# A new opening and tail for a vision block: moved steps, a load order, a last block without its means

## The chip, the core and the metric

The kernel runs on one core of a Trainium2 chip. The metric is the device time of one execution in microseconds (us). TensorE (PE) multiplies matrices and writes only to PSUM; VectorE (DVE), ScalarE (ACT) and GpSimd (POOL) work elementwise; SyncE (SP) issues most DMA transfers. The engines run their own streams of instructions and wait for each other by semaphores.

## The reference

For each of 4 images (64 channels, 64x64): a 1x1 convolution to 16 channels, batch norm and relu, then a 1x1 convolution to 9 filters for each pixel, with which the 3x3 neighbourhood of each channel is summed (`h`, 4096 tokens of width 64). Then

```
h = h + attention(layernorm(h))        # one head of width 64, softmax over 4096 keys
y = layernorm(h)
e = argmax(y @ router_w.T + router_b)  # 32 experts, the best one for each token
h = h + relu(relu(y @ W1[e] + b1[e]) @ W2[e] + b2[e])
```

All in float32.

## The kernel before

**Blocks and groups.** The tokens of an image are cut into 4 blocks of 1024 queries (BT = 8 tiles of 128), 16 blocks in all (BLOCKS), numbered through the images. A block of attention is 16 groups (PAIRS); a group scores one pair of key tiles against the 1024 queries (`score`, 16 TensorE records, two units, each followed by an exponential on ScalarE) and weighs the values with the result (`into_z`, 16 records). `usual_score(n, g)` runs one group ahead of `usual_weigh(n, g - 1)`. In blocks 0 and 1 the work is interleaved (`attention`): block 0 handles the first 8 key pairs for queries 0 and 1, so that few keys are needed early. Pairs 0 to 3 are the keys of token block 0, pairs 4 to 7 those of token block 1.

**Fills.** Everything else is a named step `name@block`, placed in a group by hand (`opening_groups` to `last_groups`; group -1 is ahead of the first). Each engine walks the same list in the same order and does its part of each step, so a step in an engine's stream holds up whatever stands behind it. `cc`, `cv`: the two convolutions for a whole image. `sum0` to `sum2`: three filter taps each on VectorE, then `ln`, the LayerNorm, which writes the keys. `xt`: the keys transposed on TensorE (`turn`), copied by ScalarE; `g`: the keys times Wq Wk, used as queries. After a block of attention: `z` (VectorE adds the two halves), `pz` (times Wv, with a 65th column for the softmax sum), VectorE divides, adds the residual and normalises to `y_block`; `yt` transposes it, `lg` makes the router's logits, `first_best` the one-hot choice, `ot` transposes that, `hid0` to `hid3` are the first layers of the 512 hidden rows with the mask of the choice, `o2` the second layer, `fin` turns the result back and `put_out` adds it to `h2`.

**Places.** A fill writes to a place in PSUM: place 0 is `both` (2 banks of 512), 7 and 8 are the two score banks, 9 is `z_ps` (`AT_THE_END`, used in the last two blocks, when attention needs them no more). `wait_free` waits until the fill that held the place before is read out.

**The end.** Block 14's experts and all of block 15's run after the last weighing. For the last block the means are taken as in every block (`normalise`: sum, centre, square, sum, a reciprocal root in eight small operations), `lg` is copied by ScalarE to `logits` before VectorE looks at it, and `o2` is accumulated in two halves of PSUM (`h` = which 64 hidden rows), which ScalarE copies and VectorE adds.

**The opening.** TensorE starts on the first image's quarter, keeps busy with `warm` matmuls on ones, and then branches on a flag (`shift_if_needed`: whether scores need a shift against overflow; here they don't). The steps behind the branch stand far off in its stream, in the Else. SP issues the loads in one order; filters go through DRAM (`store_filters`) and come back spread over the channels in three thirds (`spread_filters`), into a ring of two slots and a spare one (`chosen`). SP holds the second and third third of block 1 back until TensorE is through its branch:

```
spread_filters(1, [0])
sp.wait_ge(asked_first, 1)
spread_filters(1, [1, 2])
store_filters([2, 3])
load_image(1, 0, TILES + 2, x_loaded[1])
```

Of the kernel before, what the change touches and what calls it, by code (L numbers as in the profile page):

```python
# [17 lines left out]
D = W  # L18
# [48 lines left out]
NONE = ("sum", "ln", "pow", "z", "ask", "warm", "pre", "out")  # L67
# [5 lines left out]
AT_THE_END |= {f"{name}@{BLOCKS - 1}": k for name, k in (("hid0", 7), ("hid1", 8), ("hid2", 9), ("hid3", 7), ("o2", 8))}  # L73
# [3 lines left out]
WARM_UP, STAY_WARM, KEEP_WARM = 8, 10, 10  # L77
# [22 lines left out]

def begins(n, g):

    return g == 0 or n < 2 and g == HALF
# [48 lines left out]
def usual_groups(n):  # L152
# [5 lines left out]
                    {8: at(m, "ot"), 9: at(i, "xt"), 10: [*at(i, "g"), *at(j, "sum0 sum1")]})  # L158
    if m in CHOSEN_BY_DMA:
# [42 lines left out]
def vit_block_kernel(nc, x, once, kept, out):  # L202
# [6 lines left out]
    with ExitStack() as ctx:  # L209
# [59 lines left out]
        wv_w = sb("wv_w", [128, 130])  # L269
        wqk = sb("wqk", [64, 2, 128])  # L270
# [43 lines left out]
        lower_copied, out_ready = sem("lower_copied"), sem("out_ready")  # L314
        choices_stored, choices_loaded = sem("choices_stored"), sem("choices_loaded")
# [72 lines left out]
        def _(sp):  # L388
# [4 lines left out]
            def store_block(m):  # L393
# [3 lines left out]
                else:  # L397
                    sp.wait_ge(drained[places.of[fin]], places.nth[fin])
                for half in range(HH):
                    rows = out.rearrange("b (c h q t) w -> b q h c (t w)", c=C, h=HH, q=NQ)  # L400
                    sp.dma_start(rows[m // NQ, m % NQ, half, :, :],
                                 out_sb[half * C:(half + 1) * C, m % 2, :, :].rearrange("c t w -> c (t w)")
                                 ).then_inc(out_stored[m % 2], 16)
# [100 lines left out]
            for k in range(2):  # L504
                sp.wait_ge(out_stored[k], 32 * BLOCKS // 2)

        @block.gpsimd
        def _(pool):
# [66 lines left out]
            P.tensor_tensor(router_w[:, :], load["rm"], load["rb"], ALU.subtract)  # L575

# [8 lines left out]
        def _(pe):  # L585
# [27 lines left out]
            def turn(tiles, ident=ident):  # L613

                for j in range(BT // 2):
                    for h in range(2):
                        for a in range(2):
                            last = T.matmul(both[rows_of(a), h, j * 64:(j + 1) * 64], tiles[2 * j + a][rows_of(h)],  # L618
# [11 lines left out]

            def begin_hidden(full):
                name, i = split(full)
                wait_free(full)
                wait_drained(f"yt@{i}")
                from_both(place[places.of[full]], w1, y_t, int(name[3:]), start=True, stop=False)

            def fill(full):
# [7 lines left out]
                elif name.startswith("pre"):  # L645
                    begin_hidden(f"hid{name[3:]}@{i}")
                if name.startswith(NONE):
# [29 lines left out]
                elif name == "cv":  # L677
# [8 lines left out]
                    last.then_inc(done, 1)  # L686
                elif name in ("xt", "yt"):
# [9 lines left out]
                    last.then_inc(done, 1)  # L697
                elif name == "g":
# [10 lines left out]
                    last.then_inc(done, 1)  # L709
                elif name == "pz":  # L710
                    pe.wait_ge(z_copied, i + 1)
                    for j in range(BT // 2):
                        for c in range(2):
                            for h in range(2):
                                last = T.matmul(both[rows_of(h), c, j * 65:(j + 1) * 65],  # L715
                                                z_sb[rows_of(c), j * 128 + h * 64:j * 128 + h * 64 + 64],
                                                wv_w[rows_of(c), c * 65:(c + 1) * 65], start=True, stop=True)
                    last.then_inc(done, 1)
                elif name == "lg":
                    wait_drained(f"yt@{i}")  # L720
                    for j in range(BT // 2):
                        for r in range(2):
# [20 lines left out]
                elif name == "o2":  # L743
                    if i == BLOCKS - 1:

                        pe.wait_ge(upper_hidden, 2)

                    for part in range(2):
                        for r in range(2):
                            T.matmul(mine[rows_of(r), r, :], b2_parts[rows_of(r), part, :], onehot_t[rows_of(r), :],  # L750
                                     start=(part == 0), stop=False)
                    for f in range(FT):
                        wait_drained(f"hid{f}@{i}")
                        if i == BLOCKS - 1:
                            pe.wait_ge(upper_hidden, f + 1)
                        for h in range(2):
                            for r in range(2):
# [644 lines left out]
```

## Time and profile before

| | |
|---|---|
| median of 3 runs | 1106.2 us (1106.17 to 1106.96) |
| the profiled execution | 1105.74 us, of which the span of the trace is 1104.0 us |
| TensorE busy | 1081.4 us, 98% of the span |
| ScalarE, VectorE busy | 575.2 us, 527.7 us |
| mean granted TensorE clock | 0.995 of 2.4 GHz |

A granted clock of 1.00 is 2.4 GHz and 0.50 is 1.2 GHz. A float32 matmul has two records. Records of TensorE overlap, so the distance from start to start is what a group of them costs.

### The profile page before, as it was taken

The numbers are of one execution on the slowest core, as the hardware profiler recorded it, in microseconds if no ns is written. First come the engines' busy times: TensorE is split into PE (matmuls) and PEld (weight loads), VectorE is DVE, ScalarE is ACT, GpSimd is POOL, SyncE is SP. The second block draws the span as 40 slices with busy tenths as digits, with TensorE's granted clock in tenths as the row PEclk, the third lists the DMA queues.
The fourth block names the chain that finished last, engine by engine and source line by source line (L and its number), as shares of the span: only waits on it lengthen the run. The fifth ranks groups of instructions, "written<-read, shape, count | busy, mean of one in ns | idle before, by whom it ended". The sixth has DMA issues, their size and how long they took to land.

```text
span 1104.0 us, 28734 instructions
## 1 busy us (share of the span) xinstructions
PE 1081.4 (98%) x12492; PEld 531.2 (48%) x12492; DVE 527.7 (48%) x1039; ACT 575.2 (52%) x649; POOL 13.3 (1%) x44
## 2 busy tenths in 40 slices
PE   7799999999999999999999999999999999999997
PEld 4233333445454555435444454555555555555543
DVE  7888665436064553735546364564423131312305
ACT  2466666546555454645546454554645445464543
POOL 3100000000000000000000000000000000000000
PEclk9899999999999999999999999999999999999999
DMA  4847431113025141222313023240100101010000
GB/s 96 207 120 168 97 72 32 40 39 78 2 68 120 39 109 39 48 68 68 80 40 96 16 70 77 66 82 11 47 7 11 41 12 42 11 42 1 12 1 21
DMA packets 23377, 63.43 MB, mean 57 GB/s; under 512 B 4254, under 2 KB 8702, under 8 KB 22860
## 3 DMA queue, kind: packets, MB, share of 16 engines
q1 hardware_dynamic: 22364, 61.26, 23.3%
q8 instruction: 103, 1.69, 0.7%
q10 hardware_dynamic: 880, 0.23, 0.1%
q14 instruction: 30, 0.25, 0.1%
HBM read 52.87 MB, written 5.47 MB: 53 GB/s over the span
## 4 chain that ended last, share of the span: by engine, by line
PE 95%; DVE 1%; issue 1%; ACT 1%; DMA 1%; ACTq 0%; DVEq 0%; PEld 0%; PEldq 0%; SPq 0%
PE z_ps L787 40%; PE scores L776 38%; PE both L627 5%; PE both L758 4%; PE both L618 2%; PE both L766 1%; PE both L705 1%; PE both L724 1%; PE both L715 1%; DMA filter_ring<-filters 1%; PE both L750 0%; PE scores L627 0%; PE both L674 0%; DVE hres L1160 0%; PE z_ps L758 0%
## 5 line engine op out<-in xcount | busy, mean ns | idle before, releaser
L996 ACT ACTIVATE probs<-scores 128x1024 f32<-128x1024 f32 x512 | 496.4, 1021 | 470.7 <-PE scores L776 470.7
L776 PE MATMUL scores<-g_t,keys_t 64*64 64x512 f32 x4096 | 509.5, 591 | 1.5 <-ACT g_t L975 1.2
L787 PE MATMUL z_ps<-probs,keys 64*64 64x512 f32 x4096 | 506.8, 592 | 0.0
L776 PEld LDWEIGHTS scores<-g_t,keys_t 64*64 64x64 f32 x4096 | 210.9, 134 | 236.1 <-issue 230.1
L787 PEld LDWEIGHTS z_ps<-probs,keys 64*64 64x64 f32 x4096 | 196.4, 133 | 189.5 <-issue 178.6
L1220 DVE SCALAR_TENSOR_TENSOR hidden<-both,chosen 128x1024 f32<-128x1024 f32 x44 | 53.9, 1225 | 198.9 <-PE both L627 193.8
L1160 DVE TENSOR_TENSOR hres<-hres,tap_product 128x504 f32<-128x504 f32 (+1 forms) x128 | 88.1, 688 | 11.1 <-issue 0.9
L1148 DVE SCALAR_TENSOR_TENSOR tap_product<-filter_ring,w,xin 128x504 f32<-128x504 f32 (+1 forms) x117 | 87.0, 743 | 9.2 <-DMA filter_ring<-filters 5.5
L627 PE MATMUL both<-y_t,w 64*64 64x512 f32 x448 | 60.5, 589 | 0.0
L758 PE MATMUL both<-hidden,w 64*64 64x512 f32 x448 | 56.7, 592 | 0.0
L1261 DVE COPY o_sb<-both 128x512 f32<-128x512 f32 x14 | 9.7, 691 | 85.2 <-PE both L758 85.2
L1178 DVE COPY z_sb<-z_ps 128x512 f32<-128x512 f32 x14 | 9.7, 691 | 66.3 <-PE z_ps L787 66.3
L1128 DVE TENSOR_REDUCE stat<-logits 128x8 f32<-128x256 f32 x16 | 6.7, 419 | 62.2 <-ACT logits L981 62.2
L758 PEld LDWEIGHTS both<-hidden,w 64*64 64x64 f32 x448 | 23.9, 133 | 20.6 <-issue 19.7
L627 PEld LDWEIGHTS both<-y_t,w 64*64 64x64 f32 x448 | 21.9, 133 | 23.9 <-issue 23.4
L1249 DVE RECIPROCAL stat<-both 128x8 f32<-128x8 f32 x16 | 3.3, 208 | 57.4 <-PE both L715 57.4
L1108 DVE TENSOR_TENSOR tap_product<-tap_product 128x512 f32<-128x512 f32 x32 | 22.2, 693 | 2.4
L1110 DVE TENSOR_REDUCE stat<-tap_product 128x8 f32<-128x512 f32 x32 | 22.0, 686 | 2.3
L618 PEld LDWEIGHTS both<-w,keys 64*64 64x64 f32 x512 | 10.7, 134 | 16.1 <-issue 16.1
L618 PE MATMUL both<-w,keys 64*64 64x64 f32 x512 | 10.9, 219 | 7.4 <-DVE keys L1117 7.4
L766 PEld LDWEIGHTS both<-w,o_sb 64*64 64x64 f32 x512 | 13.1, 134 | 9.5 <-issue 9.5
L1188 DVE SCALAR_TENSOR_TENSOR out_sb<-both,h 128x256 f32<-128x256 f32 x30 | 11.3, 420 | 13.0 <-PE both L766 12.8
(162 smaller groups left out, 530.7 us busy)
## 6 DMA issues: line engine op xcount, KB each, us to landing
filter_ring<-filters SPq DMA_DIRECT2D x88, 384.0 KB, 5.4
chosen<-choices SPq DMA_DIRECT2D x44, 256.0 KB
out_dram<-out_sb SPq DMA_DIRECT2D x32, 128.0 KB, 2.4
xin<-x_dram SPq DMA_DIRECT2D x6, 528.0 KB, 9.3
g_t<-g_t SPq DMA_DIRECT2D x24, 128.0 KB, 6.2
hidden<-once_dram SPq DMA_DIRECT2D x1, 930.0 KB, 13.0
chosen<-filters SPq DMA_DIRECT2D x2, 384.0 KB, 7.3
choices<-onehot_t SPq DMA_DIRECT2D x22, 32.0 KB, 1.6
```

Source lines behind the costliest of these rows:

```text
L618: last = T.matmul(both[rows_of(a), h, j * 64:(j + 1) * 64], tiles[2 * j + a][rows_of(h)], ident[rows_of(h), rows_of(h)], start=True, stop= ...
L627: last = T.matmul(to[rows_of(c), r, :], weights[rows_of(r), cols], tokens[rows_of(r), :], start=start, stop=stop)
L758: last = T.matmul(mine[rows_of(r), h, :], w2[rows_of(h), f, :], hidden[rows_of(h), f, r, :], start=(f == 0 and h != r), stop=(f == FT - 1))
L766: last = T.matmul(both[rows_of(h), r, j * 64:(j + 1) * 64], o2_sb[rows_of(r), j * 128 + h * 64:j * 128 + h * 64 + 64], ident[rows_of(r), r ...
L776: last = T.matmul(scores[rows_of(h), c, r * 512:(r + 1) * 512], keys_t[rows_of(r), i // NQ % 2, k * 128 + 64 * h:k * 128 + 64 * h + 64], g ...
L787: last = T.matmul(z_ps[rows_of(c), h, :], keys[rows_of(h), i // NQ % 2, 2 * k + r, :], probs[rows_of(h), (2 * g + c) % RING, r * 512:(r + ...
L996: A.activation(probs[:, unit % RING, :], scores[:, c, :], ACT.Exp, scale=SCALE).then_inc(probs_ready, 1)
L1108: V.tensor_tensor(squares[:, :, :], centred[:, :, :], centred[:, :, :], ALU.mult)
L1110: V.reduce_sum(total, squares[:, :, :], AX_X)
L1148: return V.scalar_tensor_tensor(dst[:, :, lo:hi], flt, keep["b2c"][:, t:t + 1], pix, ALU.add, ALU.mult)
L1160: V.tensor_tensor(mine[:, :, lo:hi], mine[:, :, lo:hi], dst[:, :, lo:hi], ALU.add)
L1220: V.scalar_tensor_tensor(hidden[:, f, :, :], place[k][:, :, :], 0.0, chosen[:, f, :, :], ALU.max, ALU.mult).then_inc(drained[k], 1)
```

## The change

- Opening, TensorE: `KEEP_WARM` 15 instead of 10 matmuls on ones ahead of the branch; two more behind `xt@0` and three behind `g@0`, into `z_ps`. `cc@4` and `cv@4` move from groups 5 and 6 of block 0 to groups 1 and 2. In group 3 pair 2 is weighed ahead of `xt@1`, and pair 3 behind it (it was weighed in group 4, behind `g@1`).
- Opening, SP: the image of batch 1 is loaded ahead of the first stores of filters; the second third of block 1's filters no longer waits for `asked_first`.
- GpSimd makes `wv_centred`: Wv with its columns' mean taken away, and the mean as a 66th column.
- Tail: `hid0@14` is filled in group 1; `most` does the bias and three of four expert steps of `o2@14`, the fourth stands behind `yt@15` and `yu@15`, the two halves of the last `y`. `mid` takes the residual's mean ahead of time; `last_normalised` adds centred values and centred residual. `first_best` reads the logits in PSUM. `o2@15` goes to `both`, its bias (`bias`) ahead of `hid3`, each matmul over all 128 hidden rows, so that no halves are added; tokens are finished in halves (`lower_ready`, `last_out_ready`) and stored in halves.

```diff
-WARM_UP, STAY_WARM, KEEP_WARM = 8, 10, 10
+WARM_UP, STAY_WARM, KEEP_WARM = 8, 10, 15
+WAITED = PAIRS // NQ - 1
...
         0: at(1, "sum0 sum1 sum2 ln"),
-        3: at(1, "xt"),
+        1: at(NQ, "cc"),
+        2: at(NQ, "cv"),
+        WAITED: at(1, "xt"),
         4: [*at(1, "g"), *at(2, "sum0 sum1 sum2 ln")],
-        5: at(NQ, "cc"),
-        6: at(NQ, "cv"),
...
+    if n == BLOCKS - 1:
+        return merged(groups, {10: at(n, "mid")})
...
-    return merged({-1: at(m, "z"), 2: at(m, "pz"), 3: at(m - 1, "hid0 hid1 hid2 hid3 o2"), 5: at(m, "yt"),
+    return merged({-1: at(m, "z"), 1: at(m - 1, "hid0"), 2: at(m, "pz"), 3: at(m - 1, "hid1 hid2 hid3 most"), 5: [*at(m, "yt yu"), *at(m - 1, "o2")],
                    6: at(m, "lg pre0 pre1"), 7: [*at(m - 1, "fin"), *at(m, "pre2")], 8: at(m, "ot"),
-                   9: at(m, "hid0 hid1 hid2 hid3"), 10: at(m - 1, "out"), 15: at(m, "o2"), 16: at(m, "fin")})
+                   9: at(m, "hid0 hid1 hid2 bias hid3"), 10: at(m - 1, "out"), 15: at(m, "o2"), 16: at(m, "fin")})
...
+            load_image(1, 0, TILES + 2, x_loaded[1])
             store_filters([1])
-            spread_filters(1, [0])
+            spread_filters(1, [0, 1])
             sp.wait_ge(asked_first, 1)
-            spread_filters(1, [1, 2])
+            spread_filters(1, [2])
             store_filters([2, 3])
-            load_image(1, 0, TILES + 2, x_loaded[1])
...
+                    if full == "xt@0":
+                        warm(2, 256, z_ps[:, 0, :])
...
+                    if full == "g@0":
+                        warm(3, 256, z_ps[:, 0, :])
...
-                if at_once:
+                waited = n == 0 and g == WAITED
+                if at_once or waited:
+                    late = names[-1:] if waited else names
+                    for full in names[:-1] if waited else []:
+                        fill(full)
                     usual_weigh(n, g - 1)
+                    for full in late:
+                        fill(full)
+                    if waited:
+                        usual_weigh(n, g)
+                    return
...
+            def finish_last(mine):
+                for s in range(2):
+                    for f in range(FT):
+                        if s == 0:
+                            wait_drained(f"hid{f}@{BLOCKS - 1}")
+                            pe.wait_ge(upper_hidden, f + 1)
+                        for r in range(2):
+                            last = T.matmul(mine[rows_of(r), s, 0:256], w2[:, f, :], hidden[:, f, r, half_of(s)], start=False,
+                                            stop=(f == FT - 1))
+                    if s == 0:
+                        last.then_inc(lower_ready, 1)
...
+            def last_normalised(i, done):
+                V.reciprocal(rs, sums[:, :, :, D])
+                settle()
+                for a in range(2):
+                    V.tensor_tensor(rows[:, a], sums[:, a, :, 0:D], wide(rs[:, a], D), ALU.mult)
+                V.tensor_tensor(value_mean.rearrange("p (j a) -> p a j", a=2), sums[:, :, :, D + 1], rs,
+                                ALU.mult).then_inc(done, 1)
+                settle()
+                V.tensor_tensor(centred[:, :, :], centred[:, :, :], squares[:, :, :], ALU.add)
+                settle()
+                scale_of_centred()
+                for half in range(2):
+                    tiles = slice(half * BT // 2, (half + 1) * BT // 2)
+                    V.tensor_tensor(y_block[:, tiles, 1:D], centred[:, tiles, 1:D], wide(rstd[:, tiles], D - 1),
+                                    ALU.mult).then_inc(y_ready, 1)
```

## Rows read from the trace of the kernel before

**Rows 1.** The page: busy time, share of the span, instructions; then groups of instructions.
```profile
PE 1081.4 (98%) x12492; PEld 531.2 (48%) x12492; DVE 527.7 (48%) x1039; ACT 575.2 (52%) x649; POOL 13.3 (1%) x44
...
L776 PE MATMUL scores<-g_t,keys_t 64*64 64x512 f32 x4096 | 509.5, 591 | 1.5 <-ACT g_t L975 1.2
...
L618 PE MATMUL both<-w,keys 64*64 64x64 f32 x512 | 10.9, 219 | 7.4 <-DVE keys L1117 7.4
```

**Rows 2.** Timeline of TensorE, 17 to 52 us: start, length, instruction, idle before.
```profile
18.51 4.56 PE L890 MATMUL both<-ones 128*128 128x256 f32 x20
26.84 0.69 PE L618 MATMUL both<-w,keys 64*64 64x64 f32 x32 [3.76 <-DVE keys L1117]
28.32 1.99 PE L705 MATMUL both<-keys_t,a_w 64*64 64x512 f32 x8 [0.79 <-ACT keys_t L971]
31.52 4.37 PE L776 MATMUL scores<-g_t,keys_t 64*64 64x512 f32 x24 [1.22 <-ACT g_t L975]
...
47.77 0.69 PE L618 MATMUL both<-w,keys 64*64 64x64 f32 x32 [3.64 <-DVE keys L1117]
```

**Rows 3.** Chain of waits, 44 to 64 us: start, length, instruction.
```profile
48.46 3.38 PE z_ps L787 x16
51.84 1.75 PE scores L776 x16
53.59 0.86 PE both L705 x8
...
57.88 1.02 PE both L674 x16
...
62.50 0.86 PE both L684 x8
```

**Rows 4.** Windows: busy us by engine (count), granted TensorE clock, DMA share, GB/s.
```profile
11.30:16.00 4.70, 4.55 (x39) 1.51 (x38) 4.41 (x7) 2.30 (x4) 0.00 (x0) 1.00 0.01 3
28.30:30.30 2.00, 1.98 (x8) 0.32 (x8) 1.83 (x4) 0.00 (x0) 0.00 (x0) 0.50 0.95 200
48.50:51.50 3.00, 3.00 (x16) 0.98 (x12) 2.70 (x4) 0.58 (x1) 2.36 (x3) 0.50 0.38 81
```

**Rows 5.** Timeline of VectorE, 26 to 37 us.
```profile
32.56 0.74 DVE L1148 SCALAR_TENSOR_TENSOR tap_product<-filter_ring,w,xin 128x504 f32<-128x504 f32 x1 [1.92 <-DMA filter_ring<-filters]
```

**Rows 6.** Line 849, TensorE's branch: shortest, median and longest in ns.
```profile
L849 PEldq COMPARE_BRANCH  x4: 325/337/5754, 20.2 to 820.7; - x4
```

**Rows 7.** Timeline of the SP queue, 17 to 32 us: DMA issues.
```profile
18.13 9.87 SPq L442 DMA_DIRECT2D filter_ring<-filters  x4
28.05 1.24 SPq L442 DMA_DIRECT2D chosen<-filters  x2
29.33 1.62 SPq L413 DMA_DIRECT2D filters<-filters_sb  x4
```

**Rows 8.** DMA queues, 27.7 to 41.9 us: packets, MB, share.
```profile
DMA packets 631, 3.33 MB, mean 234 GB/s; under 512 B 132, under 2 KB 132, under 8 KB 503
...
q1 hardware_dynamic: 631, 3.33, 99.2%
```

**Rows 9.** DMA queues, 23.1 to 24.5 us.
```profile
q8 instruction: 1, 0.02, 5.9%
```

**Rows 10.** Timeline of VectorE, 1078 to 1088 us.
```profile
1078.18 0.69 DVE L1104 TENSOR_REDUCE stat<-h 128x8 f32<-128x512 f32 x1
...
1083.42 0.68 DVE L1117 TENSOR_TENSOR y_block<-tap_product,stat 128x504 f32<-128x504 f32 x1
...
1087.07 0.42 DVE L1128 TENSOR_REDUCE stat<-logits 128x8 f32<-128x256 f32 x1 [0.97 <-ACT logits L981]
```

**Rows 11.** Chain of waits, 1066 to 1104 us.
```profile
1081.22 3.49 PE z_ps L758 x30
...
1094.07 3.46 PE scores L758 x30
```

**Rows 12.** Timeline of the SP queue, 1098 to 1104 us.
```profile
1100.61 1.10 SPq L401 DMA_DIRECT2D out_dram<-out_sb  x2
```

More of the change, by code:

```diff
@@ L59 @@
 KEPT_AT, KEPT_N = columns(KEPT)
-NONE = ("sum", "ln", "pow", "z", "ask", "warm", "pre", "out")
+NONE = ("sum", "ln", "pow", "z", "ask", "warm", "pre", "out", "bias", "mid", "most")
 CHOSEN_BY_DMA = range(3, BLOCKS - 2)
@@ L396, in store_block @@
                     sp.wait_ge(out_ready, 1)
-                else:
+                elif m < BLOCKS - 2:
                     sp.wait_ge(drained[places.of[fin]], places.nth[fin])
[L399 to L403, printed above, removed]
+                parts = 2 if m == BLOCKS - 1 else 1
+                for part in range(parts):
+                    tiles = slice(part * BT // parts, (part + 1) * BT // parts)
+                    if parts > 1:
+                        sp.wait_ge(last_out_ready, part + 1)
+                    for half in range(HH):
+                        rows = out.rearrange("b (c h q t) w -> b q h c t w", c=C, h=HH, q=NQ)[m // NQ, m % NQ, half, :, tiles]
+                        sp.dma_start(rows.rearrange("c t w -> c (t w)"),
+                                     out_sb[half * C:(half + 1) * C, m % 2, tiles, :].rearrange("c t w -> c (t w)")
+                                     ).then_inc(out_stored[m % 2], 16)
             def store_filters(blocks):
@@ L646, in fill @@
                     begin_hidden(f"hid{name[3:]}@{i}")
+                elif name == "bias":
+                    begin_last(f"o2@{i}")
+                elif name == "most":
+                    wait_free(f"o2@{i}")
+                    begin_experts(i, place[places.of[f"o2@{i}"]])
+                    for f in range(FT - 1):
+                        add_experts(i, place[places.of[f"o2@{i}"]], f)
                 if name.startswith(NONE):
@@ L686, in fill @@
                     last.then_inc(done, 1)
+                elif full == f"yt@{BLOCKS - 1}" or name == "yu":
+                    part = 1 if name == "yu" else 0
+                    pe.wait_ge(y_ready, i + 1 + part)
+                    turn([y_block[:, t, :] for t in range(part * BT // 2, (part + 1) * BT // 2)], to=mine).then_inc(done, 1)
                 elif name in ("xt", "yt"):
@@ L744, in fill @@
                     if i == BLOCKS - 1:
[L746 to L757, printed above, removed]
[L758 to L760 removed]
+                        finish_last(mine).then_inc(done, 1)
+                        return
+                    if i != BLOCKS - 2:
+                        begin_experts(i, mine)
+                    for f in range(FT - 1 if i == BLOCKS - 2 else 0, FT):
+                        last = add_experts(i, mine, f)
+                    last.then_inc(done, 1)
+                elif i == BLOCKS - 1:
+                    pe.wait_ge(upper_hidden, FT)
+                    pe.wait_ge(lower_copied, 2)
+                    turn_back(place[places.of[f"hid3@{i}"]], 0, 2).then_inc(lower_ready, 1)
+                    wait_drained(f"o2@{i}")
+                    turn_back(mine, 2, 4).then_inc(done, 1)
                 else:
                     wait_drained(f"o2@{i}")
[L763 to L769 removed]
+                    turn_back(both, 0, 4).then_inc(done, 1)
             def score(n, g, c):
@@ L971, in drain @@
                     A.copy(in_order(keys_t[:, i // NQ % 2, i % NQ * 512:(i % NQ + 1) * 512]), turned).then_inc(done, 1)
+                elif full == f"yt@{BLOCKS - 1}" or name == "yu":
+                    A.copy(in_order(y_t[:, half_of(1 if name == "yu" else 0)]),
+                           mine[:, :, 0:128].rearrange("p h (j n) -> p h j n", n=64)).then_inc(done, 1)
                 elif name == "yt":
@@ L1180, in whole_z, with put_out @@
                     V.tensor_tensor(z_sb[:, :], z_sb[:, :], z_ps[:, 1, :], ALU.add).then_inc(z_copied, 1)
-            def put_out(i, experts):
+            def put_out(i, experts, first=0, end=BT // 2):
                 if i > 1:
@@ L1227, in drain @@
                     return
+                if full == f"fin@{BLOCKS - 1}":
+                    k = places.of[full]
+                    dve.wait_ge(lower_ready, 2)
+                    put_out(i, place[places.of[f"hid3@{i}"]][:, :, 0:128], 0, 2).then_inc(last_out_ready, 1)
+                    dve.wait_ge(filled[k], places.nth[full])
+                    put_out(i, place[k][:, :, 128:256], 2, 4).then_inc(last_out_ready, 1)
+                    return
                 if name == "out":
@@ L1244, in drain @@
                         layernorm(i)
+                elif name == "pz" and i == BLOCKS - 1:
+                    last_normalised(i, done)
                 elif name == "pz":
@@ L1258, in drain @@
                     write_normalised(y_block).then_inc(y_ready, 1)
+                elif name == "o2" and i == BLOCKS - 1:
+                    V.tensor_copy(o2_sb[:, half_of(1)], mine[:, 1, 0:256]).then_inc(done, 1)
                 elif name == "o2":
```

124 lines of the change are left out of this document (96 added, 28 removed).

## The prediction, made before the changed kernel was run

> **What bounds the kernel now.** I read four views. The page first: TensorE is busy for 1081.4 of 1104.0 us, so only its idle stretches and its slow ones can be won [rows 1]. Then its timeline over the opening: it pauses from 23.1 to 26.84 us for the first keys and from 44.1 to 47.77 us for the keys of block 1, 3.76 and 3.64 us, and the transposes of the other 14 blocks wait for nothing: the page's 7.4 us on L618 are these two pauses [rows 1, 2]. After each pause the granted clock is 0.50, that is 1.2 of 2.4 GHz: 16 weighing matmuls take 3.38 us where 16 at full clock take 1.75 [rows 3, 4]. Third the SP queue and the DMA windows, to see what the two pauses wait for. Last the chain of waits over the tail: after the last weighing TensorE, VectorE and ScalarE hand one block's work to each other for 30 us, and each handover is on the path.
>
> **The change: opening.** Three edits pull work into the second pause. In group 3 the weighing of pair 2 goes ahead of the transposes of block 1, and pair 3 behind them; cc@4 and cv@4 move from groups 5 and 6 to 1 and 2. From the first score to xt@1 TensorE then has seven units of 16 matmuls at 1.72 us (12.0), cc and cv (1.02 and 0.86 [rows 3]) and about 1.2 us for the first exponentials, 15.1 in all. Behind xt@1 the kernel after owes one weighing, cc and cv less: 1.72 + 1.02 + 0.86 = 3.6 us. If scores began at 30.7 us, xt@1 would begin at 45.8, and score 4 at 45.8 + 0.7 + 1.72 = 48.2 instead of 51.84 [rows 3]: 3.6 + 3.6 = 7.2 us.
>
> The keys of block 1 must be there: they come at 47.6 us now, but VectorE lost 1.92 us waiting for the second third of its filters [rows 5], issued only when TensorE has taken its branch (asked_first). The change issues that third before. That gives 45.7 us. GpSimd's dozen new small operations run beside it; I allow 0 to 1 us. The image of batch 1 is loaded ahead of all this, into a stretch in which the DMA share is 0.01 [rows 4]: hidden, 1.08 MB at 234 GB/s being 4.6 us [rows 8]. ScalarE's copy of cv@4 waits until the filters of blocks 2 and 3 are stored, with the exponentials queued behind it. SP issues those stores at 29.3 now [rows 7] and some 2 us later then; ScalarE comes to the copy after 40 us: no cost. Later blocks keep their slack, as nothing there waits now [rows 1].
>
> What speaks against it is the branch. TensorE's branch at L849 took 5.75 us the first time and 0.34 otherwise [rows 6]. It begins at 20.2; the first filter transfers, issued from 18.13 [rows 7], fill the DMA queues, and the 16 KB block of instructions comes only in the window from 23.1 to 24.5 us, when they are through [rows 9]. From 27.7 to 41.9 us all 631 packets are the kernel's own, and not one is of instructions [rows 8]. So I take it that a fetch waits behind what is queued before it. Two more transfers of 384 KB will stand there, issued at 19.3 and 19.9, just ahead of the branch: 1.7 us each at 234 GB/s. Bounds: 0 and 3.4 us. I take 2.0, one whole and a bit of the other, since the second is issued nearly together with the branch. xt@0 then starts at 28.8 instead of 26.84.
>
> The Trainium skill bears on this twice. "Runtime: NRT & Kernel Launch", Instruction fetch mechanics, says that a taken branch whose target isn't held forces a DMA fetch before execution goes on; the 5.75 us agree. "DMA: Bandwidth & Descriptors", Queues, rings and completion order, says that each DMA engine goes round its queue rows packet by packet, by which a fetch would wait only its turn and the added transfers would cost nothing; rows 8 and 9 rather look like a queue served in order, and the sum would be 1096 by the page.
>
> The clock. The warm-up matmuls grow from 10 to 15, 0.456 us each (20 records in 4.56 us [rows 2]), so they end at 24.9. With xt@0 at 26.84 the pause is 1.9 us, and the shortest pause after which the clock fell is 3.64 [rows 2]: it would stay. With xt@0 at 28.8 the pause is 3.9 us, and I expect 1.2 GHz again. The fillers added behind xt@0 (two) and g@0 (three) then cost double: 1.8 and up to 2.7 us where ScalarE's copies (0.6 and 1.0 us) are the only reason to wait. Added up: xt@0 28.8 to 29.5, fillers to 31.3, g@0 (1.99 us at low clock [rows 2]) to 33.3, three fillers, the clock rising in them as TensorE is busy without a gap, to 34.3. Scores at 34.3 instead of 31.52; xt@1 at 49.4, with no wait for keys; score 4 at 51.8. Opening: 0.0 + 3.6 = 3.6 us, or 4.7 if the clock rises a matmul group earlier. I take 4.1.
>
> **The change: tail.** Times are those of the trace before.
> - hid0@14 (about 1.3 us) moves into TensorE's pause of 1.64 us before pz; pz stays where it is.
> - The mean of the last LayerNorm goes: one reduction and one centring, from 1078.18 in steps of 0.77 [rows 10], 1.53 us; a small operation for the values' mean comes in (0.2), and the first half of y is written in 0.37 instead of 0.68. y is half ready at 1082.4 instead of 1084.1 [rows 10]. The residual's sum (mid) is made in group 10, where VectorE has nothing else to do.
> - TensorE has by then done three of four expert steps of block 14 (3.49 us for four [rows 11]). Both halves are turned and copied by 1083.8; the fourth step (0.86) and the logits (0.70) end at 1084.9.
> - VectorE must first add o2@14, behind ScalarE's copy: 1084.2 + 0.6 + 0.7 = 1085.5. So the maximum over logits starts at 1085.55, not 1087.07 [rows 10]: 1.5 us. The copy of the logits (0.4) is saved, but the o2 addition takes its place. The place of the logits is now freed by VectorE's comparison, at 1086.5; fin@14 and pre2 wait behind that on TensorE and are through by 1088.2, before the one-hot transposes at 1088.45.
> - The next steps are unchanged up to hid3. The bias matmuls (0.43) move ahead of hid3 into TensorE's wait; the 16 expert matmuls keep their 3.46 us [rows 11] if two column groups run side by side. If they don't, it is 3.4 more. No row here has a matmul over all rows and half the columns; the nearest are those on quarters of the array, which do overlap (C below), so I take 3.43.
> - The copy plus addition of o2 (1.4) shrink to a copy of half a tile (0.4), and one half is turned back and put out under the other. The last put_out ends 2.1 us earlier. But SP now issues four transfers at 0.55 each instead of two in 1.10 [rows 12]: first at 1098.05, last done at 1100.3 instead of 1101.7. 1.4 us are left.
> Tail: 1.5 + 1.4 = 2.9 us (2.2 to 3.6).
>
> Sum: 4.1 + 2.9 = 7.0 us. The profiled execution took 1105.74 us (span 1104.0 and 1.7 around it), giving 1098.7; the median of the three runs is 0.46 higher, giving 1099.2. I call less than 0.2% (2.2 us) no difference.
>
> **The rivals.**
> - A, the fetch isn't held up (by the rule above). For: TensorE's branch might be asked for before the second pair has reached the queues. Then the clock stays at 2.4 GHz, scores start at 30.7, and the opening gives 7.2 (6.2 if GpSimd slows VectorE, whose keys are then needed to the tenth). 1106.2 - 7.2 - 2.9 = 1096.1.
> - B, my forecast: 1099.2; from 1097.5 to 1101.5 with the delay between 1.7 and 3.4 us and the clock early or late.
> - C, the column groups of the last experts run one after the other: 3.4 us dearer, 1102.6 with B. Against it: the eight records of g@1 (L705) take 0.86 us together, though a record of 512 columns alone is put at 0.59 [rows 1, 3].
> - D, slower: a second block of instructions, needed some twenty matmuls into the scores, is caught behind the last third of the filters and the 930 KB of weights, as in the 14 us without a fetch [rows 8]. 1.7 MB at 234 GB/s are 7.5 us in which TensorE would stand still: 1106.7 with a delay of 2.0 us and up to 1109. It decides once TensorE is held up by more than 7 us beyond B. Against it: the same load stood behind the branch before, with 1.08 MB of image more, and TensorE didn't stand still.
> - E, no gain: VectorE runs out of instructions or filters in block 1, so that its keys come 3 us later than I say, and the tail gives half. 1104 to 1106.
>
> **How the numbers follow.** A 0.30, B 0.46, C 0.08, D 0.05, E 0.11. The likeliest gives 1099.2. A's lower edge (1095.2) and C and half of E (to 1103.5) are taken into the range, which leaves out D and the rest of E. B alone is 1097.5 to 1101.5. Faster: A, B, C and a little of E, 0.86; within 0.2%: most of E and part of D, 0.10; slower: 0.04.
>
> **What would show it.** In the profile after: L849's longest branch (over 5.75 us: B; the same: A), and xt@0 at 28.8 or 26.8; the granted clock in g@0's stretch; no idle time on TensorE before xt@1; score 4 at 51.8 or 48.2 with no cc or cv behind it; VectorE's filter wait of 1.92 us gone. In the tail: the maximum over logits 1.5 us sooner behind the last weighing; the last experts in 3.4 or 6.9 us; four stores issued back to back. It would be wrong if instructions arrive in another order than I read from the windows, or if column groups don't overlap.

## The result and the profile after

| | before | after |
|---|---|---|
| median, same chip | 1106.48 us (5 runs, 1106.17 to 1107.66) | 1100.87 us (5 runs, 1099.41 to 1101.23) |
| ratio | | 0.9947 (95% interval 0.9933 to 0.996) |
| profiled execution, and its span | 1105.74, 1104.0 us | 1100.87, 1099.1 us |

The change makes the kernel 5.6 us faster (4.4 to 7.4 by the interval); 7.0 was forecast, and 1100.87 lies in the range of 1095.2 to 1103.5. The page shows that it isn't less work. TensorE is busy 5.0 us longer than in [rows 1], and idle for 12.7 us of its span instead of 22.6: 9.9 - 5.0 = 4.9 us, by which the two spans differ.

```profile
PE 1086.4 (99%) x12516; PEld 536.5 (49%) x12516; DVE 528.8 (48%) x1045; ACT 574.7 (52%) x649; POOL 17.2 (2%) x54
L872 PE MATMUL scores<-g_t,keys_t 64*64 64x512 f32 x4096 | 507.9, 590 | 0.3 <-ACT probs L1107 0.3
```

**Opening.** TensorE's timeline, to be laid beside [rows 2] (start, length, instruction, idle before):

```profile
19.29 8.41 PE L995 MATMUL both<-ones 128*128 128x256 f32 x30
31.02 1.14 PE L650 MATMUL both<-w,keys 64*64 64x64 f32 x32 [3.32 <-issue]
32.09 2.07 PE L995 MATMUL z_ps<-ones 128*128 128x256 f32 x4
34.09 1.09 PE L803 MATMUL both<-keys_t,a_w 64*64 64x512 f32 x8
35.11 1.56 PE L995 MATMUL z_ps<-ones 128*128 128x256 f32 x6
36.60 1.99 PE L872 MATMUL scores<-g_t,keys_t 64*64 64x512 f32 x16
...
51.30 0.65 PE L650 MATMUL both<-w,keys 64*64 64x64 f32 x32
51.77 1.90 PE L883 MATMUL z_ps<-probs,keys 64*64 64x512 f32 x16
53.49 1.90 PE L872 MATMUL scores<-g_t,keys_t 64*64 64x512 f32 x16
```

`xt@0` (the transposes of the first keys) starts at 31.02, where 28.8 was forecast. "issue" in front of it says that no engine and no transfer was late: TensorE itself wasn't there. From `xt@0` to the first scores it takes 5.58 us (5.5 forecast), from there to `xt@1` 14.7 (15.1), and `xt@1` waits for nothing. The 5.5 came true by other parts: `g@0` costs 1.0 us and not 1.99, the transposes, and the fillers behind them and behind `g@0`, 1.1 more together. Score 4 begins at 53.49 against 51.84 in [rows 3]; what follows it is 3.6 us shorter. So the opening gives 3.6 - 1.65 = 1.95 us and not 4.1.

VectorE's wait for the second third of its filters [rows 5] is gone, but another stands behind it, for the last third (`chosen`), which SP issues only when TensorE has taken its branch. VectorE's timeline:

```profile
37.18 0.74 DVE L1273 SCALAR_TENSOR_TENSOR tap_product<-chosen,w,xin 128x504 f32<-128x504 f32 x1 [1.33 <-DMA chosen<-filters]
...
46.95 0.68 DVE L1231 TENSOR_TENSOR keys<-tap_product,stat 128x504 f32<-128x504 f32 x1
```

So the keys of block 1 are ready at 47.63, as late as before (47.6), where 45.7 was forecast. It costs nothing only because TensorE comes to them at 51.30.

Line 945 is the branch (line 849 in [rows 6]): shortest, median and longest in ns, then the start of the first.

```profile
L945 PEldq TENSOR_LOAD <-flag x4: 301/310/490, 23.5 to 818.1; - x4
L945 PEldq COMPARE_BRANCH  x4: 323/336/6042, 24.4 to 818.7; - x4
```

The branch begins at 24.4 instead of 20.2. The DMA queues from 27.4 to 29.0 us show its instructions (q8) arriving as the filters (q1) run out, as in [rows 9], but 4.4 us later:

```profile
q8 instruction: 1, 0.02, 6.0%
q1 hardware_dynamic: 8, 0.01, 2.3%
```

The granted clock (after the busy time of POOL, ahead of the DMA share) is 0.50, that is 1.2 GHz, in the middle of the warm-up and again behind the pause, and full again for `g@0` and the second lot of fillers:

```profile
20.50:23.50 3.00, 3.00 (x9) 2.37 (x8) 2.68 (x5) 0.00 (x0) 2.31 (x7) 0.50 0.97 227
30.70:34.00 3.30, 2.98 (x36) 2.15 (x36) 3.04 (x5) 0.58 (x1) 0.00 (x0) 0.50 0.61 152
34.10:36.50 2.40, 2.40 (x15) 1.25 (x14) 1.65 (x3) 1.01 (x1) 0.00 (x0) 1.00 1.00 256
```

**Tail.** From the chain of waits:

```profile
1069.77 2.16 PE z_ps L883 x20
...
1082.96 0.69 DVE o_sb L1431
...
1088.49 0.44 PE both L680 x8
...
1090.14 3.63 PE both L691 x32
1093.77 0.02 issue
1093.79 0.44 DVE o_sb L1424
```

The last weighing ends at 1071.93 and the span at 1099.1: 27.2 us. In the trace before it is 1073.91 and 1104.0: 30.1 us, from this line of its chain of waits:

```profile
1070.46 3.45 PE z_ps L787 x32
```

The tail gives 2.9 us, as forecast. VectorE's maximum over the logits, to compare with [rows 10]:

```profile
1083.57 0.42 DVE L1247 TENSOR_REDUCE stat<-both 128x8 f32<-128x256 f32 x1
```

Counted from the end of the last weighing that is 1085.55 on the clock of the trace before; 1085.55 was forecast. The experts take 3.63 us (3.43 forecast), so the column groups do overlap: 0.11 us for a record of 256 columns, where one of the warm-up, over the whole array, took 0.23 [rows 2].

1.95 + 2.9 = 4.85 us of the 4.9 by which the spans differ.

### The profile page after: what moved, and what is told of

It is laid out like the page before. It is cut to its first block, busy times and chain, and to the rows that moved or that the text cites. A ratio compares the mean times of both kernels' runs of the same rounds, so it can differ in the third digit from the quotient of the medians.

```text
span 1099.1 us, 28810 instructions
## 1 busy us (share of the span) xinstructions
PE 1086.4 (99%) x12516; PEld 536.5 (49%) x12516; DVE 528.8 (48%) x1045; ACT 574.7 (52%) x649; POOL 17.2 (2%) x54
## 3 DMA queue, kind: packets, MB, share of 16 engines
q1 hardware_dynamic: 22524, 61.26, 23.7%
## 4 chain that ended last, share of the span: by engine, by line
PE 98%; issue 1%; ACT 1%; DVE 0%; DVEq 0%; POOL 0%; ACTq 0%; POOLq 0%
PE z_ps L883 40%; PE scores L872 39%; PE both L659 5%; PE both L709 4%; PE both L650 2%; PE both L995 1%; PE both L668 1%; PE both L803 1%; PE both L817 1%; PE both L828 1%; PE both L701 1%; PE scores L659 0%; PE both L764 0%; PE z_ps L709 0%; PE both L691 0%
## 5 line engine op out<-in xcount | busy, mean ns | idle before, releaser
L709 PEld LDWEIGHTS both<-hidden,w 64*64 64x64 f32 x448 | 23.9, 133 | 20.6 <-issue 19.7
L659 PEld LDWEIGHTS both<-y_t,w 64*64 64x64 f32 x448 | 21.9, 133 | 23.9 <-issue 23.5
L1079 ACT COPY keys_t<-both 128x512 f32<-128x512 f32 x16 | 9.5, 594 | 13.7 <-PE both L650 13.7
```

The lines of the kernel that those rows point to most:

```text
L659: last = T.matmul(to[rows_of(c), r, :], weights[rows_of(r), cols], tokens[rows_of(r), :], start=start, stop=stop)
L709: last = T.matmul(to[rows_of(r), h, :], w2[rows_of(h), f, :], hidden[rows_of(h), f, r, :], start=(f == 0 and h != r), stop=(f == FT - 1))
```

## The experiments

Two questions come first: does the branch wait for the transfers queued ahead of it, and which part of the opening postpones TensorE? Unless said otherwise an edit is made in the kernel after. Medians of before on the three chips: 1106.20, 1106.49 and 1106.42 us.

**1. Ten warm-up matmuls again** (`w10`), and **the load order of before** (`ask_order`), and both (`w10_ask_order`), and nothing queued ahead of the branch (`no_load`).

```diff
 # w10
-WARM_UP, STAY_WARM, KEEP_WARM = 8, 10, 15
+WARM_UP, STAY_WARM, KEEP_WARM = 8, 10, 10
 # ask_order; no_load leaves the first spread_filters out and has spread_filters(1) behind the wait
-            spread_filters(1, [0, 1])
+            spread_filters(1, [0])
             sp.wait_ge(asked_first, 1)
-            spread_filters(1, [2])
+            spread_filters(1, [1, 2])
```

> The kernel after with 10 warm-up matmuls ahead of the branch instead of 15, nothing else. Three theories of why the first transposes came at 31.0 us. Q, queue depth: TensorE's stream runs only about 16 matmul records ahead of the array, so a longer warm-up postpones the flag load (23.5 us after, 19.3 before); with 10 it is back at 19.3 to 20.1. F, the fetch behind the branch waits until the filter transfers queued ahead of it (now four, to 27.6 us) are through: the branch still ends at about 30 us and lasts some 10 us, the time stays within 1 us of the kernel after. L, the branch has a fixed length of 5.8 to 6.0 us whatever is queued: it ends at 26 to 27 us, the transposes start at 27 to 28, and the time falls by 3 us or a little more.

> The kernel after with the second third of block 1's filters held back behind asked_first again, 15 warm-up matmuls kept. Q: the flag load stays at 22 to 23.5 us. F: the two transfers ahead are through by 24.3 us, so the branch, started at 23 to 24.4, finds empty queues and lasts 3 us: the transposes start at 27.5 to 28. L: the branch lasts 6 us as before and the transposes start at 29 to 31. The keys of block 1 come 1 to 2 us later than in the kernel after (47.6 us) by F as well as by L. Time: F 1 to 3 us faster than after, L 0 to 1 slower.

> Both undone: 10 warm-up matmuls and only the first third ahead of the branch, as in the kernel before. Q, F and L all say a branch from 20.2 (plus up to 0.8) that lasts 5.8 us, and transposes at 26.8 to 27.6. Then scores at about 31.5 to 32.5, the wait for the keys of block 1 at 47.6 us short (0 to 1 us) and, if so, a time 2.5 to 4 us below the kernel after, near 1097.5.

> The kernel after with all three thirds of block 1's filters behind asked_first: nothing but the small stores is queued when TensorE branches; 15 warm-up matmuls kept. F: the branch lasts 3 us or less. L: it lasts 5.8 to 6.0 us. Q: it starts at 22 to 24.4 us either way. By F the transposes start at 27 to 27.5; VectorE then waits for its filters and the keys of block 1 come at 51 to 53 us, so the time is 1 to 3 us above the kernel after.

Measured, from the profiles of all runs (us). A third of the filters is two transfers of 384 KB; "ahead" is how many of them SP had issued when TensorE took its branch; "from the first issue" counts from SP's issue of the first of them to the arrival of the instructions. `after` and `after_again`, `w10` and `w10_again` are executions of one kernel. `tail_alone` and `opening_alone` belong to part 2, `w10_no_fillers` and `w10_whole_store` to part 3.

| | branch starts | ahead | its instructions arrive | from the first issue | branch takes | xt@0 | median | ratio |
|---|---|---|---|---|---|---|---|---|
| no_load | 23.8 | 0 | 24.8 | | 3.46 | 27.89 | 1104.80 | 0.9986 (0.9976 to 0.9995) |
| before | 20.2 | 2 | 23.1 | 5.0 | 5.75 | 26.84 | 1106.48 | |
| tail_alone | 20.2 | 2 | 23.1 | 4.8 | 5.68 | 26.95 | 1103.53 | 0.9975 (0.9965 to 0.9985) |
| w10_ask_order | 21.0 | 2 | 23.4 | 4.8 | 5.26 | 26.88 | 1099.50 | 0.9934 (0.9917 to 0.995) |
| ask_order | 22.7 | 2 | 23.7 | 4.9 | 3.84 | 27.49 | 1100.81 | 0.9952 (0.9936 to 0.9969) |
| w10 | 20.5 | 3 | 24.9 | 6.4 | 7.24 | 28.39 | 1096.97 | 0.9911 (0.9895 to 0.9928) |
| w10_again | 20.3 | 3 | 24.8 | 6.4 | 7.28 | 28.22 | 1098.15 | 0.9924 (0.9911 to 0.9936) |
| w10_no_fillers | 20.6 | 3 | 25.2 | 6.5 | 7.32 | 28.54 | 1099.96 | 0.9937 (0.9921 to 0.9954) |
| w10_whole_store | 20.7 | 3 | 25.3 | 6.6 | 7.44 | 28.85 | 1099.46 | 0.9931 (0.9908 to 0.9954) |
| w12 | 22.1 | 4 | 27.1 | 8.9 | 7.54 | 30.30 | 1101.14 | 0.9953 (0.994 to 0.9966) |
| after | 24.4 | 4 | 27.5 | 8.6 | 6.04 | 31.02 | 1100.87 | 0.9947 (0.9933 to 0.996) |
| after_again | 24.0 | 4 | 26.9 | 8.6 | 5.62 | 30.19 | 1099.96 | 0.994 (0.9928 to 0.9952) |
| after_look | 23.7 | 4 | 26.6 | 8.4 | 5.80 | 30.12 | 1098.58 (1 run) | |
| opening_alone | 24.2 | 4 | 27.0 | 8.4 | 5.76 | 30.57 | 1103.92 | 0.9972 (0.9959 to 0.9984) |

The instructions arrive when the last transfer queued ahead of the branch is through. Counted from the first issue that is after 4.8 to 5.0 us with two transfers ahead, 6.4 to 6.6 with three and 8.4 to 8.9 with four, though the branch began anywhere from 20.2 to 22.7 with two ahead and from 22.1 to 24.4 with four. The branch ends 2.5 to 3.0 us after they arrive. With nothing ahead they arrive 1.0 us after the branch began, and it takes 3.46 us. That is the floor here. `ask_order` comes near it (1.0 and 3.84), since its branch begins when the second transfer is nearly through: 31 filter packets are still to come in the 0.9 us behind 22.7. What SP issues behind the branch doesn't hold the fetch up. So the prediction's reading of the queue stands, and rival A falls.

Of the theories in the expectations, Q held: in `w10` the load of the flag is back at 19.7. L is out, as the branch takes from 3.46 to 7.54 us. F, the wait behind the queue, holds, but had `w10`'s branch end near 30 behind four transfers; it ends at 27.8 behind three. Three times missed: `ask_order` was to be 1 to 3 us faster than after and isn't; `w10_ask_order` was to come near 1097.5 and took 1099.50, its `xt@1` waiting 2.20 us for the keys; `no_load` was to be 1 to 3 us slower than after and is 3.9 slower.

What `ask_order` buys at the branch it loses at the keys: VectorE's filters come later, and TensorE waits for `xt@1`, as [rows 2] had it. TensorE's timeline of `ask_order`:

```profile
27.49 0.69 PE L650 MATMUL both<-w,keys 64*64 64x64 f32 x32 [1.65 <-DVE keys L1231]
...
48.23 0.69 PE L650 MATMUL both<-w,keys 64*64 64x64 f32 x32 [1.65 <-DVE keys L1231]
```

and of `no_load`, where the wait costs more than the opening gives (the tail alone gives 3.0, the kernel gains 1.4):

```profile
53.34 1.13 PE L648 MATMUL both<-w,keys 64*64 64x64 f32 x32 [6.30 <-DVE keys L1229]
```

The surprise is `w10`: without the five added warm-up matmuls the kernel gains 9.2 us on before instead of 5.6. Its branch starts at 20.5, and its `xt@0` at 28.39 is the prediction's case (28.8) nearly to the letter: one added transfer stands ahead of the fetch, and SP was still issuing the other when the branch was taken.

**2. The parts alone, in the kernel before.** `tail_alone` is before with everything of the change behind the opening, `opening_alone` before with the new opening (warm-up, fillers, order of groups, load order).

> The kernel before with the new tail only (opening, load order, warm-up and group 3 of the kernel before). From the end of the last weighing to the end of the span the kernel before takes 30.1 us and the kernel after 27.2. If the tail is worth what that says, 2.9 us: 1103.3, ratio 0.9974. The opening should look as before: branch 5.8 us from 20.2, transposes at 26.8, a wait of 3.6 us ahead of block 1's transposes. Rival: the end of the trace flatters it, and less than 1.5 us come back in the time.

> The kernel before with the new opening only (15 warm-up matmuls, fillers, load order, cc and cv in groups 1 and 2, pair 2 weighed ahead of xt@1), old tail. In the two profiles the start of score 4 moved from 51.84 to 53.49 us with 3.6 us of work less behind it, so 2.0 us: 1104.2, ratio 0.998. It should again show the flag load at 22 to 24 us and transposes at 29 to 31 us. Rival: the opening gives more in most executions than in that profiled one, in which the clock fell in the warm-up; then 3 to 4 us.

Measured: `tail_alone` 1103.53 us (9 runs), 0.9975 (0.9965 to 0.9985), 3.0 us; `opening_alone` 1103.92 (6 runs), 0.9972 (0.9959 to 0.9984), 2.6 us. They add up to 5.6 us, the change's gain; the intervals (1.7 to 3.9 and 1.8 to 4.5 us) leave room for a small effect of one part on the other. The tail is worth its forecast, and the opening is where the missing 1.5 to 2.2 us are. From the end of the last weighing to the end of the span it is 30.1 us in both profiles with the old tail, and 27.2 in all eleven with the new one and its stores in halves.

**3. What the fillers are worth, and the stores in halves.** Both with ten warm-up matmuls. `w10_no_fillers` leaves the five fillers out; `w10_whole_store` stores the last block with two transfers instead of four.

```diff
 # w10_no_fillers
-                    if full == "xt@0":
-                        warm(2, 256, z_ps[:, 0, :])
...
-                    if full == "g@0":
-                        warm(3, 256, z_ps[:, 0, :])
 # w10_whole_store
-                parts = 2 if m == BLOCKS - 1 else 1
+                parts = 1
+                if m == BLOCKS - 1:
+                    sp.wait_ge(last_out_ready, 2)
...
-                sp.wait_ge(out_stored[k], 32 * (BLOCKS // 2 + k))
+                sp.wait_ge(out_stored[k], 32 * BLOCKS // 2)
```

> 10 warm-up matmuls, and no fillers behind xt@0 and g@0. Theory that fillers cost: TensorE arrives at 28.4 at 1.2 GHz either way, two fillers and three fillers delay g@0 by 0.5 to 1.1 us and the scores by 0 to 1 us; without them the time is up to 1.5 us below that of 10 warm-up matmuls alone (1097.0). Theory that they pay: without them the clock stays low 3 to 7 us longer into the scores and it costs 1 to 2 us more: 1098 to 1099.

> 10 warm-up matmuls, and the last block stored by two transfers of 128 KB behind the last put_out, where the kernel after issues four of 64 KB. The four keep SP at 0.6 us each until 1.8 us behind the last put_out; two would be issued within 1.1 us of it. Theory that SP's issues set the end: whole is 0.3 to 0.5 us sooner from the last put_out to the end of the span (3.5 us instead of 3.8). Theory that halving helps by overlapping: whole is 0.5 us later. Too little for the timed runs, so the spans of the profiles decide.

Measured: `w10_no_fillers` 1099.96 us (4 runs, 1098.88 to 1100.75), 0.9937 (0.9921 to 0.9954), against 1096.97 and 1098.15 with fillers, on other chips. Its clock stays at 1.2 GHz for 10.2 us (28.4 to 38.7), against 3.4 us behind the branch in both profiles of `w10`, and though nothing stands between `g@0` and the scores, score 4 begins at 52.41, 1.4 us later than in `w10` (51.04):

```profile
30.46 1.99 PE L800 MATMUL both<-keys_t,a_w 64*64 64x512 f32 x8 [0.79 <-ACT keys_t L1074]
33.66 6.13 PE L867 MATMUL scores<-g_t,keys_t 64*64 64x512 f32 x32 [1.21 <-ACT g_t L1081]
```

32 score records take 6.06 us to the next start where they take 4.2 in `w10`. But `w10_whole_store`, the only kernel with ten warm-up matmuls and fillers on the same chip, took 1099.46 us, its runs overlap with those without fillers, and its clock was low for 6.8 us (27.5 to 34.4). Its score 4:

```profile
52.43 1.90 PE L874 MATMUL scores<-g_t,keys_t 64*64 64x512 f32 x16
```

Behind the branch's pause the clock was at 1.2 GHz for 6.8, 6.8 and 10.2 us in the three profiles without fillers (`before`, `tail_alone`, `w10_no_fillers`), and for 0, 3.4 or 6.8 us in the eleven with them, after pauses of 0.9 to 5.2 us. So the fillers, which I had priced only as a cost, may well pay, as TensorE works through its two short waits; against a scatter as wide as this one pair of profiles doesn't show by how much, and the runs on one chip don't show it at all.

`w10_whole_store` took 1099.46 (4 runs, 1096.37 to 1101.65), 0.9931 (0.9908 to 0.9954): too wide to tell 0.4 us. The profiles can. SP's queue in `w10`, then in `w10_whole_store` (start, length over all stores; four and two of them are of the last half block):

```profile
1089.22 5.51 SPq L419 DMA_DIRECT2D out_dram<-out_sb  x6
```

```profile
1090.55 4.83 SPq L421 DMA_DIRECT2D out_dram<-out_sb  x4
```

From the end of the last `put_out` to the end of the span it is 3.77 us in `w10` (1092.93 to 1096.7) and 3.36 with whole stores (1094.24 to 1097.6). From the last weighing it is 27.2 and 26.8 us, and 27.2 in every other profile with halves. The halves cost 0.4 us: SP's four issues of 0.5 to 0.6 us are the chain there, and they begin too late to save anything.

**4. After, ten and twelve matmuls on one chip.** The gain of `w10` rested on four runs, and the kernel after scatters.

> The kernel after, unchanged, beside w10_again and w12 on one chip, because its opening scatters more from execution to execution than that of the kernel before. Both theories: 1100.9, from 1099.5 to 1102.5.

> The kernel after with ten warm-up matmuls instead of fifteen ahead of the branch. Theory Q (the added matmuls stand ahead of the flag load and postpone the branch): 2 to 4 us below the kernel after on the same chip, 1097 to 1099. Rival (the first measurement was a lucky phase of the clock, and the warm-up costs nothing, as the prediction had it): within 0.7 us of the kernel after.

> Twelve warm-up matmuls. Theory Q: the flag load comes some 1 us later than with ten (two more matmuls, 0.46 us each at the full clock, twice that at the low one), so the time lies between the two, 1098 to 1100. Rival (the clock's phase decides and not the place of the load): anywhere from 1097 to 1102 and not in order.

Measured: after 1099.96 (6 runs, 1098.25 to 1101.51), `w10_again` 1098.15 (5 runs, 1097.03 to 1098.86), `w12` 1101.14 (5 runs, 1100.4 to 1101.68); ratios in the table. Ten is again the fastest, by 1.8 us, a little under the 2 to 4 that I had expected. Twelve isn't between: it is the slowest. Theory Q hadn't that; the rival, that the clock decides, had allowed any order. The table gives the larger part of the answer: it is not the warm-up's own time that counts but what SP issues meanwhile. SP's queue in `w10_again`, the branch, and the DMA queues from 24.7 to 26.2 us:

```profile
18.35 2.38 SPq L460 DMA_DIRECT2D filter_ring<-filters  x4
```

```profile
L945 PEldq COMPARE_BRANCH  x4: 322/336/7282, 20.3 to 816.1; - x4
```

```profile
q1 hardware_dynamic: 61, 0.31, 92.6%
q8 instruction: 1, 0.02, 5.8%
```

The fourth transfer is issued in the last quarter of 18.35 to 20.73, the branch begins at 20.32, and the instructions arrive at 24.75 while 61 packets of filters are still passing. The same three views of `w12`, the last from 27.0 to 28.4 us:

```profile
18.14 2.38 SPq L460 DMA_DIRECT2D filter_ring<-filters  x4
```

```profile
L945 PEldq COMPARE_BRANCH  x4: 323/336/7537, 22.1 to 819.0; - x4
```

```profile
q8 instruction: 1, 0.02, 5.5%
q1 hardware_dynamic: 2, 0.00, 0.1%
```

All four were issued by 20.5, the branch begins at 22.1, and the instructions come when not a filter is left. Two more matmuls (0.9 us at full clock) cost 2.1 us of `xt@0` (28.22 to 30.30); three further ones cost nothing, because the fetch waits for the same transfer. The clock has the rest: score 4 begins 2.86 us later in `w12` than in `w10_again` (53.73 and 50.87), and the 0.8 us beyond the 2.1 come with 6.8 us at 1.2 GHz where `w10_again` had 3.4.

**5. Why the kernel after has two times.** Its six executions in part 4 were 1098.25, 1098.51, 1098.83, and 1101.10, 1101.35, 1101.51.

> One more look at the kernel after, whose executions on the last chip lay in two groups, 1098.3 to 1098.8 and 1101.1 to 1101.5, both profiles so far being of the upper one. Theory P: what parts the groups is the granted clock behind the first keys, and an execution near 1098.5 shows less than 3.4 us at 1.2 GHz between 26 and 40 us, with the fetch of instructions still behind all four transfers, near 27 us. Rival: such an execution has the fetch ahead of the fourth transfer, near 25 us. If the execution falls near 1101 again, it shows 3.4 or 6.8 us at 1.2 GHz and a fetch near 27 us, and the two groups stay open.

Measured: 1098.58 us, an execution of the lower group. TensorE's timeline, and two windows of it:

```profile
30.12 0.69 PE L650 MATMUL both<-w,keys 64*64 64x64 f32 x32 [3.25 <-issue]
30.75 1.13 PE L995 MATMUL z_ps<-ones 128*128 128x256 f32 x4
31.81 1.09 PE L803 MATMUL both<-keys_t,a_w 64*64 64x512 f32 x8
32.83 1.56 PE L995 MATMUL z_ps<-ones 128*128 128x256 f32 x6
34.32 1.95 PE L872 MATMUL scores<-g_t,keys_t 64*64 64x512 f32 x16
...
51.18 1.90 PE L872 MATMUL scores<-g_t,keys_t 64*64 64x512 f32 x16
```

```profile
27.00:29.50 2.50, 0.00 (x0) 0.00 (x0) 2.34 (x4) 0.00 (x0) 0.00 (x0) 1.00 0.00 0
29.50:33.00 3.50, 2.88 (x45) 1.64 (x46) 3.18 (x6) 0.62 (x2) 0.00 (x0) 1.00 0.36 112
```

The branch (23.7, 5.80 us) and `xt@0` are where they were, but the clock never falls behind the pause. From `xt@0` to the scores it is 4.20 us against 5.58 after 3.4 us at 1.2 GHz, and 6.91 in `after_again`, with 6.8 us at 1.2 GHz. That is 2.7 of the 2.8 us between the spans of these two executions. So the clock can part the groups; that it parts them all isn't shown. There is one profile in the lower group, the whole opening can also begin late (by 0.8 us in the profile after), and the mean granted clocks don't part as the times do: 0.997, 0.997 and 0.998 in the lower group, 0.994, 0.994 and 0.997 in the upper. Here score 4 begins at 51.18, which makes the opening worth 4.3 us.

## Why the prediction was right, and what it missed

- **The fetch waits behind what is queued ahead of it** (rivals A and B): right, shown by the table. By the rule of the Trainium skill ("DMA: Bandwidth & Descriptors", Queues, rings and completion order), that a DMA engine takes the queue rows in turn, packet by packet, the added transfers would have been free. The runs disagree: the instructions arrived at 23.1 to 23.7, 24.8 to 25.3 and 26.6 to 27.5 us with two, three and four transfers ahead. Why the two kinds of packets don't take turns isn't shown.
- **The delay of 2.0 us**: this step failed. It chose "one whole and a bit of the other, since the second is issued nearly together with the branch", with the branch at 20.2. But the warm-up of 15 matmuls stands ahead of the flag's load in the same stream. TensorE's sequencer takes the load only when 16 or 17 records of the warm-up are left (23.5 with the array busy to 27.7; the flag was ready at 20.0, and ScalarE read it then). The prediction wrote of the longer warm-up only when it would end. With the branch at 22 or later both transfers are ahead of it, and the delay is the upper bound, 3.4 us: 26.84 + 3.4 = 30.2, measured 30.12 to 30.30 in three profiles. (The branch itself ends 3.6 to 3.8 us later there than before. Some 0.3 of that is hidden: before, `xt@0` began 0.9 us behind the branch, waiting for VectorE's keys, and now 0.6.) With ten matmuls and the new load order the delay is 1.4 to 2.0 us, and the step is right as written. In the profile after, 31.02, another 0.8 us comes from ahead of the warm-up, which begins at 19.29 instead of 18.51; in `after_again` and `after_look`, the same kernel, it begins at 18.71, so this is scatter between executions. So `xt@0` is 2.2 us late, 1.4 for the delay and 0.8 for the late beginning; 0.5 us of that come back on the way to score 4, since the exponentials and the transposes of block 1 cost less than allowed. The opening is worth 1.95 instead of the 3.6 that the prediction's times gave; the other 0.5 of its 4.1 was taken for a clock that might rise early.
- **The end of the warm-up**: the prediction's sum is off. Five more matmuls of 0.456 us behind 23.1 end at 25.4 and not at 24.9, so by its own `xt@0` of 28.8 the pause is 3.4 us, shorter than any after which it had seen the clock fall. The warm-up ended at 27.70: the late beginning adds 0.8, and 3.4 us at 1.2 GHz inside the warm-up add 1.6 (30 records in 8.41 us; 6.72 in `ask_order`, where the clock stayed up). The clock fell inside the warm-up in ten of the fourteen profiles; the prediction hadn't this.
- **The clock falls behind a pause of 3.9 us, and would not behind 1.9**: it fell, but behind a pause of 3.32, and the rule was too simple. After a pause of 3.25 us (`after_look`) it stayed at 2.4 GHz, after 3.07 (`after_again`) it fell, and so it did in `tail_alone`, without fillers, after 2.07 and a further gap of 0.79. After 1.65 and 1.76 us (`ask_order`, `w10_ask_order`) it stayed, and after 2.20 ahead of `xt@1` in `w10_ask_order` it fell. That the forecast 5.5 us from `xt@0` to the scores came out is luck in part, as the parts show.
- **The wait of VectorE for its second third is gone, `xt@1` doesn't wait**: right, and `ask_order` and `no_load` show that this third is what the opening lives on. "That gives 45.7 us" was wrong: the wait for the last third, 1.33 us in the profile after and 1.80 in `after_look`, takes the gain back, because that third is held up with the branch. In `w10` and `w10_again`, with earlier branches, there is no such wait and the keys come at 46.2 and 45.9. The image of batch 1 ahead of all is hidden: `cc` and `cv` in their new groups had no wait in the profile after, and in `after_again` and `after_look` the warm-up begins within 0.2 us of before.
- **The 3.6 us of work pulled forward**: right. It can be read in `after_look`, where score 4 is 0.66 us earlier than in [rows 3] with cc, cv and a weighing already done.
- **Tail, 1.5 and 1.4 us**: right in sum and in both terms. In the second the experts cost 0.2 more than the forecast, and four stores instead of two cost 0.4 that the step had allowed for.
- **Rivals C, D, E**: the 32 expert records of 128 rows by 256 columns take 3.63 us and not 6.9 (C); after the branch's own block the next blocks of instructions came without idle time on TensorE, at 31.7 and 38.2 us in the profile after (D); the keys were in time (E).

What stays open: what decides, from execution to execution, whether and for how long the clock falls, which is worth 2.7 us between two profiles of the kernel after, and how much the fillers give.

## What to carry to other kernels

Work that only keeps an engine warm is not free when it stands ahead of a load, a branch or a wait in that engine's stream: look up when the instruction behind it will be taken, and what other queues issue in the meantime. Here a first taken branch costs 3.5 us alone, and each 384 KB that SP had queued ahead of it and that isn't through adds its own time (some 1.6 us for the third, 2.1 for the fourth), so put the branch ahead of the transfers, or count them. When a forecast moves an event (here the branch), redo every step that had used its old time. The best kernel of the study is the one after with ten warm-up matmuls, 8.3 and 9.2 us faster than before on two chips; the same with whole stores gained 7.0 on a third.

## What the runs showed of the hardware

- TensorE's sequencer runs some 16 matmul records ahead of the array here: in all profiles 16 or 17 records of the warm-up were left when the flag's load was taken. It came 0.0 to 0.4 us after the flag was ready with 10 warm-up matmuls, 2.1 us with 12 and 1.9 to 3.6 us with 15 (1.9 where the clock stayed at 2.4 GHz).
- A fetch of instructions waits for the transfers queued ahead of the branch: 4.8 to 5.0, 6.4 to 6.6 and 8.4 to 8.9 us from the first issue with two, three and four of 384 KB, wherever the branch began (20.2 to 22.7 us with two, 22.1 to 24.4 with four).
- From the arrival of a block of instructions to the end of the branch it is 2.5 to 3.0 us, whatever the branch had waited.
- The same kernel was at 1.2 GHz for 0, 3.4 and 6.8 us behind the branch in three executions, after pauses of 3.25, 3.32 and 3.07 us.
- Matmuls over 128 rows in two column groups overlap: 32 records of 256 columns in 3.63 us, 0.11 each, against 0.23 for a record of 256 columns over the whole array.
